# Exponentials of key tiles taken in pairs, and four elementwise steps moved from ScalarE to VectorE, in an attention and gathered-expert kernel

## Chip, cores and metric

The kernel runs on all 8 cores of one Trainium2 chip. Each core computes 4 of the 32 sequences, with no exchange between cores. The metric is the device time in microseconds of the slowest core.

## What is computed

For each sequence `x` (2048 tokens of 1024 features) a layer has two halves:

```
q = x @ Wq + bq (8 heads of 128);  k, v = x @ Wkv + bkv (one head, shared)
q += pe; k += pe
probs = softmax(causal(q k^T / sqrt(128)));  attn = probs @ v
x = layernorm(x + attn @ Wo)

grouped = x in groups of 32 tokens
logits = grouped @ Wc + bc + tie;  perm = (logits == max over the 32 tokens)
permuted = perm^T @ grouped                      (128 expert slots per group)
result = relu(permuted @ W1 + b1) @ W2 + b2, scattered back with perm
x = layernorm(x + result)
```

## The kernel before

One program is written out for five engine queues, with waits on counting semaphores; nothing is scheduled by a tool, so each engine runs its instructions in the order in which `build_nc` emits them. `wait(engine, mark)` makes the next instruction of an engine wait for a count, `gset` stores the count after which a buffer is free, and `gwait` waits for it. The loop over the 4 sequences runs these stages:

- **Projections** (L308 to L347): q, k, v for the whole sequence stay in SBUF.
- **Attention**, four blocks `qb` of 512 query rows (L451 to L547). Block `qb` uses the first 4, 8, 12 or 16 key tiles of 128 keys (`kcmax`), and its last four tiles cross the diagonal. Per head and key tile `kc`: `emit_scores` (L459) is one TensorE matmul into the PSUM bank `pp_s[kc % 2]`; `emit_exp` (L467) is a ScalarE exponential from that bank to `pT[kc % 2]`; on the four diagonal tiles VectorE multiplies `pT` by a mask (L475); `emit_pv` (L491) is four matmuls of 129 columns that add `pT` times `v` (and the row sum) into two PSUM banks. Both `pp_s` and `pT` have two buffers. Scores run two tiles ahead: in the loop of L541 to L547, `emit_pv(kc)` is followed by `emit_scores(kc + 2)` and `emit_exp(kc + 2)`.
- **End of a head**: VectorE takes four reciprocals of the row sums (L506), ScalarE scales the four 128x128 results into `pTn` (L513). TensorE transposes them (L524) after the first two score matmuls of the next head, and VectorE copies them to `atT` (L529).
- **Output projection and layernorm** at the end of each block, four row tiles of 128 tokens: 16 matmuls (L568), VectorE adds `x` (L576) and sums (L582), ScalarE squares (L586, L589), then `ln_tile` computes mean and deviation in small VectorE steps with one ScalarE square root (L382), and ScalarE applies the norm to the 128x1024 tile (L396).
- **Logits** per block: ScalarE casts the four tiles to bf16 (L417), TensorE transposes them (L426) and multiplies by `Wc` (L440).
- **Experts**, four quarters `q4` of 256 features: for each row tile `tt` ScalarE casts 256 columns of `x2` to bf16 (`x2b`, two buffers, L679), eight small matmuls gather the tokens (L690) and VectorE and ScalarE cast two results each to `gq` (L701). Then the W1 matmuls (L721), later the W2 matmuls (L775), a restack through device memory and the scatter (L831, L838). A second layernorm (L868) and the store end the sequence.

The waits that matter below are these lines of `emit_scores` and `emit_exp`:

```python
gwait("tensor", ("ps", ping))
if kc >= 2:
    wait("tensor", exp_m[kc - 2])
...
wait("scalar", sv)
gwait("scalar", ("pT", ping))
```

The first pair says that a score matmul needs its bank read by the exponential of two tiles ago. The second says that an exponential needs its scores, and that the PV matmuls of two tiles ago have read its output buffer.

Of the kernel before, what the change touches and what calls it, by code (L numbers as in the profile page):

```python
# [26 lines left out]
def build_nc(cfg):  # L27
# [88 lines left out]
    pT = [at(f"pT{i}", [128, 512], BF16, r4 + T * 2 + NT * 132 * 2 + i * 1024)  # L116
          for i in range(2)]
# [21 lines left out]
    pp_s = [nc.alloc_psum_tensor(f"pp_s{i}", [128, 512], F32).ap() for i in range(2)]  # L139
# [115 lines left out]
    def emit_ln2_finish():  # L255
        mred = now("sDVE")
        wait("scalar", mred)
        wait("scalar", now("sACT"))
        gwait("scalar", ("pT", 0)); gwait("scalar", ("pT", 1))
        for tt in range(NT):  # L260
            if tt > 0:
                wait("scalar", now("sACT"))
            inc("scalar", "sACT", 1, lambda e, tt=tt: e.activation(
                out=pT[0][:, :], in_=x2[:, tt * 1024: tt * 1024 + 512],
                func=AF.Square, accum_out=st_v[:, tt: tt + 1]))
            inc("scalar", "sACT", 1, lambda e, tt=tt: e.activation(
                out=pT[1][:, :], in_=x2[:, tt * 1024 + 512: tt * 1024 + 1024],
                func=AF.Square, accum_out=st_r[:, tt: tt + 1]))
        sq2 = now("sACT")
        gset(("pT", 0), sq2); gset(("pT", 1), sq2)  # L270
        bv = emit_ln_stats_finish()
        wait("scalar", bv)
        wait("scalar", now("sACT"))
        return bv

    for s in range(NSEQ):
# [88 lines left out]
        def ln_tile(tt, sq):  # L365
# [86 lines left out]
        for qb in range(NQB):  # L452
# [10 lines left out]
            def emit_exp(h, kc, sv, exp_m, mask_m):  # L463
                ping = kc % 2
                wait("scalar", sv)
                gwait("scalar", ("pT", ping))
                ev = inc("scalar", "sACT", 1, lambda e, ping=ping: e.activation(  # L467
                    out=pT[ping][:, :], in_=pp_s[ping][:, :], func=AF.Exp,
                    bias=c_negC, scale=cfg.SCALE))
                exp_m[kc] = ev  # L470
                gset(("ps", ping), ev)
                j = kc - 4 * qb
                if j >= 0:
                    wait("vector", ev)
                    mv = inc("vector", "sDVE", 1, lambda e, ping=ping, j=j: e.tensor_tensor(  # L475
                        pT[ping][:, :], pT[ping][:, :],
                        c_zl[:, (3 - j) * 128: (3 - j) * 128 + 512], ALU.mult))
                    mask_m[kc] = mv
# [20 lines left out]
            def emit_epilogue_pre(h):  # L499
# [54 lines left out]
            for t4 in range(4):  # L554
# [19 lines left out]
                if qb == 0 and t4 == 0 and s > 0:  # L574
# [89 lines left out]
        for q4 in range(4):  # L664
# [337 lines left out]
```

How the kernel before makes its waits and increments, by code:

```python
    def inc(eng, sem, n, buildfn):  # L160
        cnt[sem] += n; v = cnt[sem]
        emit(eng, lambda e, b=buildfn, s=sem, n=n: b(e).then_inc(sems[s], n))
        return (sem, v)
# [1 line left out]
    def wait(eng, mark):  # L165
        if mark is None: return
        sem, v = mark
        emit(eng, lambda e, s=sem, v=v: e.wait_ge(sems[s], v))
```

## Time and profile before

| | us |
|---|---|
| median of 2 runs | 5027.58 (5018.58 to 5036.58) |
| profiled execution | 5022.15 |
| its span on the slowest core | 5020.6 |
| spans of the 8 cores | 4982.2 to 5020.6 |

The profile is one execution, read on the slowest core. A busy TensorE (PE) is not an array at its peak, since its matmuls overlap and their ends are modelled. "Clock" is the TensorE clock that was granted, as a share of 2.4 GHz; it has the two levels 0.5 and 1.0, and an average over a stretch lies between. In the timeline an instruction with x2 or x4 is a run of equal ones, with the time of the whole run. "Idle before" is the time for which an engine stood before an instruction, with what ended it.

### The profile page before, as it was taken

How to read it: one execution, taken by the hardware profiler on the slowest of the kernel's cores; microseconds unless marked ns; L12 is line 12 of the kernel's file. 1: busy time of each engine (PE TensorE's matmuls, PEld its weight loads, DVE VectorE, ACT ScalarE, POOL GpSimd, SP SyncE). 2: the span in 40 equal slices, each digit the busy share in tenths (PEclk: the TensorE clock that was granted, in tenths of full speed). 3: DMA queues.
4: the chain of work that ended last, by engine and by line, in shares of the span. 5: the costliest groups of instructions: out<-in, count | busy, mean ns of one | idle time of the engine just before them, and what ended most of it. 6: DMA issues, size and time to landing. Idle time of an engine off the chain costs nothing.

```text
span 5020.6 us, 66002 instructions; the slowest of 8 cores (4982.2 to 5020.6 us)
## 1 busy us (share of the span) xinstructions
PE 2644.8 (53%) x19792; PEld 1424.3 (28%) x19792; DVE 1550.1 (31%) x4169; ACT 1883.5 (38%) x3892; POOL 18.2 (0%) x35
## 2 busy tenths in 40 slices
PE   4666664523376656462446666555426566646431
PEld 1333333311132223251113332233213223324310
DVE  1322225412232222442233212244332322134322
ACT  0345552311325556231133555433112445633313
POOL 0000000000000000000000000000000000000000
PEclk9677876555566778565566677755557678866555
DMA  4200015277400000107731000102772000010474
GB/s 87 59 13 5 18 28 125 64 163 154 118 29 14 17 18 9 68 18 168 151 105 43 17 2 17 59 35 62 156 136 97 17 17 18 1 59 35 93 160 134
DMA packets 174965, 325.00 MB, mean 65 GB/s; under 512 B 5670, under 2 KB 137126, under 8 KB 169130
## 3 DMA queue, kind: packets, MB, share of 16 engines
q1 hardware_dynamic: 26474, 164.01, 10.8%
q10 hardware_dynamic: 140224, 117.45, 10.6%
q0 software_dynamic: 7936, 39.33, 4.6%
q8 instruction: 184, 3.01, 0.2%
q14 instruction: 147, 1.20, 0.1%
HBM read 240.01 MB, written 120.07 MB: 72 GB/s over the span
## 4 chain that ended last, share of the span: by engine, by line
PE 40%; ACT 19%; DMA 17%; issue 12%; DVE 11%; ACTq 1%; DVEq 0%; SPq 0%; POOL 0%; POOLq 0%
PE pp_pv L491 8%; ACT pT L467 7%; DMA rp_scratch<-rpn 7%; DMA rpe<-rp_scratch 7%; PE pp_s L459 6%; PE pp_s L308 5%; PE pp_w L568 4%; PE pp_s L721 4%; PE pp_s L690 3%; PE pp_s L775 2%; ACT x2b L679 2%; ACT pTn L513 2%; DVE pT L475 2%; PE pp_tr L426 2%; DVE rpn L788 1%
## 5 line engine op out<-in xcount | busy, mean ns | idle before, releaser
L467 ACT ACTIVATE pT<-pp_s,c_negC 128x512 bf16<-128x512 f32 x1280 | 845.1, 690 | 350.5 <-PE pp_pv L491 210.6
L491 PE MATMUL pp_pv<-vS,pT 128*128 128x129 bf16 x5120 | 618.1, 257 | 379.5 <-DVE pT L475 229.9
L491 PEld LDWEIGHTS pp_pv<-vS,pT 128*128 128x128 bf16 x5120 | 392.8, 112 | 777.5 <-issue 773.1
L459 PE MATMUL pp_s<-qT,kT 128*128 128x512 bf16 x1280 | 599.3, 487 | 0.1
L475 DVE TENSOR_TENSOR pT<-pT,c_zl 128x512 bf16<-128x512 bf16 x512 | 217.7, 425 | 962.4 <-ACT pT L467 961.3
L775 PE MATMUL pp_s<-w_2t,inr 32*64 32x256 bf16 x1024 | 139.8, 400 | 572.6 <-DVE rpn L788 473.1
L308 PE MATMUL pp_s<-xT,w_q 128*128 128x512 bf16 x1024 | 251.2, 414 | 282.9 <-DMA w_kv<-cwkv 214.0
L788 ACT CAST rpn<-pp_s 128x256 bf16<-128x256 f32 x256 | 95.3, 372 | 700.7 <-DMA rpe<-rp_scratch 612.1
L568 PE MATMUL pp_w<-w_o,atT 128*128 128x512 bf16 x1024 | 285.4, 442 | 108.7 <-DVE x L576 94.3
L788 DVE CAST rpn<-pp_s 128x256 bf16<-128x256 f32 x256 | 108.7, 425 | 600.2 <-DMA rpe<-rp_scratch 519.7
L690 PE MATMUL pp_s<-pmt,x2b 32*128 32x128 bf16 x1024 | 128.4, 281 | 269.5 <-ACT x2b L679 259.7
L775 PEld LDWEIGHTS pp_s<-w_2t,inr 32*64 32x64 bf16 x1024 | 71.9, 122 | 638.0 <-issue 637.4
L467 ACT ACT_TABLE_LOAD x16 | 20.5, 1283 | 583.6 <-PE pp_s L459 583.6
L513 ACT ACTIVATE pTn<-pp_pv,rs 128x128 bf16<-128x128 f32 x512 | 146.1, 367 | 244.2 <-DVE rs L506 237.5
L721 PE MATMUL pp_s<-gq,w 128*32 128x64 bf16 x4096 | 228.3, 416 | 17.5 <-ACT gq L701 6.9
L701 ACT CAST gq<-pp_s 128x256 bf16<-128x256 f32 x256 | 95.2, 372 | 355.6 <-PE pp_pv L690 334.1
L308 PEld LDWEIGHTS pp_s<-xT,w_q 128*128 128x128 bf16 x1024 | 106.8, 105 | 426.0 <-issue 363.3
L721 PEld LDWEIGHTS pp_s<-gq,w 128*32 128x32 bf16 x4096 | 211.3, 144 | 32.2 <-issue 28.7
L426 PE MATMUL pp_tr<-c_ident,casttile 128*128 128x128 bf16 x512 | 74.8, 300 | 246.0 <-ACT casttile L417 169.4
L701 DVE CAST gq<-pp_s 128x256 bf16<-128x256 f32 x256 | 108.7, 425 | 262.8 <-PE pp_s L690 260.0
L679 ACT ACTIVATE x2b<-x 128x256 bf16<-128x256 f32 x256 | 109.2, 427 | 213.5 <-DVE pmT L649 120.8
L568 PEld LDWEIGHTS pp_w<-w_o,atT 128*128 128x128 bf16 x1024 | 108.2, 110 | 282.2 <-issue 212.7
(95 smaller groups left out, 3123.4 us busy)
## 6 DMA issues: line engine op xcount, KB each, us to landing
rp_scratch<-rpn SPq DMA_DIRECT2D x32, 2048.0 KB, 17.4
rpe<-rp_scratch ACTq DMA_DIRECT2D x32, 2048.0 KB, 22.4
xtile<-x SPq DMA_DIRECT2D x64, 512.0 KB, 3.7
y<-x SPq DMA_DIRECT2D x64, 512.0 KB, 4.4
w<-cw ACTq DMA_DIRECT2D x12, 2048.0 KB, 8.5
w_2t<-cw ACTq DMA_DIRECT2D x48, 512.0 KB, 13.0
xT<-xT POOLq DMA_DIRECT2D x4, 4096.0 KB, 27.6
w<-w POOLq DMA_DIRECT2D x4, 2048.0 KB, 16.2
```

The source lines that it names most:

```text
L308: mmq = inc("tensor", "sPE", 1, lambda e, ps=ps, c=c, hc=hc, tb=tb: e.matmul(ps[:, :], w_q[:, c * 1024 + hc * 128: c * 1024 + hc * 128 + 128],
L459: return inc("tensor", "sPE", 1, lambda e, kc=kc, ping=ping, h=h, qb=qb: e.matmul(pp_s[ping][:, :], kT[:, kc * 128: kc * 128 + 128], qT[:, ...
L467: ev = inc("scalar", "sACT", 1, lambda e, ping=ping: e.activation(out=pT[ping][:, :], in_=pp_s[ping][:, :], func=AF.Exp, bias=c_negC, scal ...
L475: mv = inc("vector", "sDVE", 1, lambda e, ping=ping, j=j: e.tensor_tensor(pT[ping][:, :], pT[ping][:, :], c_zl[:, (3 - j) * 128: (3 - j) * ...
L491: ping=ping, sub=sub, kc=kc, kcmax=kcmax: e.matmul(bank[:, colo: colo + 129], pT[ping][:, sub * 128: sub * 128 + 128], vS[:, kc * 132: kc ...
L513: e.activation(out=pTn[:, sub * 128: sub * 128 + 128], in_=bank[:, colo: colo + 128], func=AF.Identity, scale=rs[:, sub: sub + 1]))
L568: wv = inc("tensor", "sPE", 1, lambda e, h=h, half=half, t4=t4: e.matmul(pp_w[:, half * 512: half * 512 + 512], atT[:, h * 512 + t4 * 128: ...
L679: cm2 = inc("scalar", "sACT", 1, lambda e, tt=tt, q4=q4: e.activation(out=x2b[tt % 2], in_=x2[:, tt * 1024 + q4 * 256: tt * 1024 + q4 * 25 ...
L690: gvv = inc("tensor", "sPE", 1, lambda e, j=j, cc=cc, tt=tt, bidx=bidx: e.matmul(banks4g[bidx][:, cc * 128: cc * 128 + 128], x2b[tt % 2][j ...
L721: cc=cc, q4=q4: e.matmul(ps[b * 32: b * 32 + 32, qq * 64: qq * 64 + 64], w_1[q4 % 2][:, cc * 4096 + es * 32: cc * 4096 + es * 32 + 32], ba ...
L775: q4=q4: e.matmul(ps[half * 64: half * 64 + 64, 0:256], inr[b * 32: b * 32 + 32, q * 64: q * 64 + 64], w_2t[0][b * 32: b * 32 + 32, q * 25 ...
L788: m = inc(eng2, sem2, 1, lambda e, r=r, ps=ps, cp3=cp3: cp3(e)(rpn[:, r * 256: r * 256 + 256], ps[:, 0:256]))
```

## The change

Four things are changed:

1. `pT` and `pp_s` become the two halves of one tile each (`pTp`, `pp_sp`, 1024 columns), and one exponential of 128x1024 takes two key tiles at once (`emit_exp_pair`). It needs both score matmuls, and both halves of `pTp` free. The loop goes by pairs: two score matmuls of the next pair, then the PV matmuls of this pair, then the next exponential.
2. The scaling of the head's results (L513) goes from ScalarE to VectorE.
3. The layernorm apply after the output projection (L396) goes from ScalarE to VectorE.
4. The cast to `x2b` (L679) goes from ScalarE to VectorE.

```diff
-    pT = [at(f"pT{i}", [128, 512], BF16, r4 + T * 2 + NT * 132 * 2 + i * 1024)
-          for i in range(2)]
+    pTp = at("pTp", [128, 1024], BF16, r4 + T * 2 + NT * 132 * 2)
+    pT = [pTp[:, 0:512], pTp[:, 512:1024]]
...
-            wait("scalar", bv)
-            wait("scalar", now("sACT"))
-            am = inc("scalar", "sACT", 1, lambda e, tt=tt: e.activation(
...
-                func=AF.Identity, scale=st_r[:, tt: tt + 1], bias=st_b[:, tt: tt + 1]))
+            wait("vector", now("sDVE"))
+            am = inc("vector", "sDVE", 1, lambda e, tt=tt: e.tensor_scalar(
...
+                st_r[:, tt: tt + 1], st_b[:, tt: tt + 1], ALU.mult, ALU.add))
...
+            def emit_exp_pair(h, kc, sv, exp_m, mask_m):
                 wait("scalar", sv)
+                gwait("scalar", ("pT", 0)); gwait("scalar", ("pT", 1))
+                ev = inc("scalar", "sACT", 1, lambda e: e.activation(
+                    out=pTp[:, :], in_=pp_sp[:, :], func=AF.Exp,
                     bias=c_negC, scale=cfg.SCALE))
+                exp_m[kc] = ev; exp_m[kc + 1] = ev
+                gset(("ps", 0), ev); gset(("ps", 1), ev)
+                for k2 in (kc, kc + 1):
...
-                    nm = inc("scalar", "sACT", 1, lambda e, bank=bank, colo=colo, sub=sub:
...
+                    nm = inc("vector", "sDVE", 1, lambda e, bank=bank, colo=colo, sub=sub:
+                             e.tensor_scalar(pTn[:, sub * 128: sub * 128 + 128],
...
-                for kc in range(kcmax):
-                    epi["pv_last"] = emit_pv(h, kc, kcmax, exp_m, mask_m)
-                    nxt = kc + 2
-                    if nxt < kcmax:
-                        sv = emit_scores(h, nxt, exp_m)
-                        emit_exp(h, nxt, sv, exp_m, mask_m)
+                for kc0 in range(0, kcmax, 2):
+                    sv = None
+                    if kc0 + 2 < kcmax:
+                        emit_scores(h, kc0 + 2, exp_m)
+                        sv = emit_scores(h, kc0 + 3, exp_m)
+                    epi["pv_last"] = emit_pv(h, kc0, kcmax, exp_m, mask_m)
+                    epi["pv_last"] = emit_pv(h, kc0 + 1, kcmax, exp_m, mask_m)
+                    if sv is not None:
+                        emit_exp_pair(h, kc0 + 2, sv, exp_m, mask_m)
...
-                gwait("scalar", ("x2b", tt % 2))
-                cm2 = inc("scalar", "sACT", 1, lambda e, tt=tt, q4=q4: e.activation(
...
+                gwait("vector", ("x2b", tt % 2))
+                cm2 = inc("vector", "sDVE", 1, lambda e, tt=tt, q4=q4: e.tensor_copy(
```

The order on TensorE in the middle of a head of block 1, on tiles off the diagonal. `sACT` is ScalarE's count, `sDVE` VectorE's; L459 is a score matmul, L491 a PV matmul. Before, two buffers `pT_77` and `pT_78` take turns:

```order
L491 MATMUL pp_pv<-vS,pT_77 128x129 [waits sACT]
L491 MATMUL pp_pv<-vS,pT_77 128x129 x3
L459 MATMUL pp_s<-qT,kT 128x512 [waits sACT]
L491 MATMUL pp_pv<-vS,pT_78 128x129 [waits sACT]
L491 MATMUL pp_pv<-vS,pT_78 128x129 x3
L459 MATMUL pp_s<-qT,kT 128x512 [waits sACT]
```

And in the changed kernel:

```order
L459 MATMUL pp_sp<-qT,kT 128x512 [waits sACT] x2
L491 MATMUL pp_pv<-vS,pTp 128x129 [waits sACT]
L491 MATMUL pp_pv<-vS,pTp 128x129 x3
L491 MATMUL pp_pv<-vS,pTp 128x129 [waits sACT]
L491 MATMUL pp_pv<-vS,pTp 128x129 x3
```

The two score matmuls of the next pair now stand ahead of the eight PV matmuls of this pair, and both groups wait for the same exponential.

The order on VectorE at the end of a head of block 0 (L506 reciprocals, L475 masks, L529 the copy of the transposed result). Before:

```order
L506 RECIPROCAL rs<-pp_pv 128x1 x3
L475 TENSOR_TENSOR pT_77<-pT_77,c_zl 128x512 [waits sACT]
L475 TENSOR_TENSOR pT_78<-pT_78,c_zl 128x512 [waits sACT]
L529 COPY atT<-pp_tr 128x512 [waits sPE]
```

And in the changed kernel:

```order
L506 RECIPROCAL rs<-pp_pv 128x1 x3
L513 TENSOR_SCALAR pTn<-pp_pv,rs 128x128 [waits sDVE]
L513 TENSOR_SCALAR pTn<-pp_pv,rs 128x128 x3
L475 TENSOR_TENSOR pTp<-pTp,c_zl 128x512 [waits sACT] x2
L529 COPY atT<-pp_tr 128x512 [waits sPE]
```

The four scalings stand behind the reciprocals on VectorE, and no longer ahead of the next head's exponential on ScalarE.

The order on ScalarE in the gather stage (L679 makes `x2b` of a row tile, L701 casts gathered results). Before:

```order
L679 ACTIVATE x2b_88<-x_64 128x256 [waits sPE]
L701 CAST gq<-pp_s 128x2x128 [waits sPE]
L701 CAST gq<-pp_pv 128x2x128 [waits sPE]
L679 ACTIVATE x2b_89<-x_64 128x256 [waits sPE]
```

And on VectorE in the changed kernel, where L678 makes `x2b` and L699 casts:

```order
L678 CAST x2b_88<-x_64 128x256 [waits sPE]
L699 CAST gq<-pp_sp 128x2x128 [waits sPE]
L699 CAST gq<-pp_pv 128x2x128 [waits sPE]
L678 CAST x2b_87<-x_64 128x256 [waits sPE]
```

The cast of the next row tile stands behind two gather casts as before, but in VectorE's queue.

## Rows read from the trace of the kernel before

**Rows 1.** The page: span, and busy time of the engines.
```profile
span 5020.6 us, 66002 instructions; the slowest of 8 cores (4982.2 to 5020.6 us)
...
PE 2644.8 (53%) x19792; PEld 1424.3 (28%) x19792; DVE 1550.1 (31%) x4169; ACT 1883.5 (38%) x3892; POOL 18.2 (0%) x35
```

**Rows 2.** Windows: attention blocks 0 to 3 of the first sequence: window, busy per engine, clock.
```profile
155.00:213.00 58.00, 34.89 (x190) 17.90 (x188) 19.06 (x69) 29.69 (x61) 1.03 (x2) 0.52 0.34 91
265.00:351.00 86.00, 56.55 (x349) 29.56 (x348) 19.88 (x68) 51.08 (x93) 0.00 (x0) 0.70 0.00 1
401.00:513.00 112.00, 74.86 (x510) 39.44 (x509) 19.88 (x68) 71.89 (x125) 0.00 (x0) 0.80 0.00 1
564.00:701.00 137.00, 92.20 (x666) 49.11 (x665) 19.93 (x68) 93.11 (x157) 0.00 (x0) 0.85 0.00 1
```

**Rows 3.** Groups: instruction, shapes, count | busy us, mean ns | idle before, releaser.
```profile
L467 ACT ACTIVATE pT<-pp_s,c_negC 128x512 bf16<-128x512 f32 x1280 | 845.1, 690 | 350.5 <-PE pp_pv L491 210.6 <-PE pp_s L459 134.4 <-issue 1.0
...
L475 DVE TENSOR_TENSOR pT<-pT,c_zl 128x512 bf16<-128x512 bf16 x512 | 217.7, 425 | 962.4 <-ACT pT L467 961.3
...
L513 ACT ACTIVATE pTn<-pp_pv,rs 128x128 bf16<-128x128 f32 x512 | 146.1, 367 | 244.2 <-DVE rs L506 237.5 <-PE pp_s L459 6.7
...
L788 DVE CAST rpn<-pp_s 128x256 bf16<-128x256 f32 x256 | 108.7, 425 | 600.2 <-DMA rpe<-rp_scratch 519.7 <-PE pp_s L775 77.6
...
L396 ACT ACTIVATE x<-x,st_b,st_r 128x1024 f32<-128x1024 f32 x64 | 79.4, 1240 | 62.2 <-DVE st_b L392 62.2
...
L582 DVE TENSOR_REDUCE st_m<-x 128x1 f32<-128x1024 f32 x64 | 78.1, 1220 | 6.6
...
L417 ACT ACTIVATE casttile<-x 128x1024 bf16<-128x1024 f32 x64 | 62.0, 1039 | 0.0
```

**Rows 4.** Timeline (start, us, engine, instruction), block 3, inner loop, fast TensorE clock.
```profile
1938.81 1.26 ACT L467 ACTIVATE pT<-pp_s,c_negC 128x512 bf16<-128x512 f32 x2 [0.36 <-PE pp_pv L491]
...
1939.65 0.39 PE L491 MATMUL pp_pv<-vS,pT 128*128 128x129 bf16 x4 [0.44 <-ACT pT L467]
...
1939.88 0.38 PE L459 MATMUL pp_s<-qT,kT 128*128 128x512 bf16 x1
...
1940.41 1.26 ACT L467 ACTIVATE pT<-pp_s,c_negC 128x512 bf16<-128x512 f32 x2 [0.33 <-PE pp_s L459]
```

**Rows 5.** Timeline, block 3, inner loop, slow TensorE clock.
```profile
4341.55 0.69 ACT L467 ACTIVATE pT<-pp_s,c_negC 128x512 bf16<-128x512 f32 x1 [0.45 <-PE pp_pv L491]
...
4342.38 0.59 PE L491 MATMUL pp_pv<-vS,pT 128*128 128x129 bf16 x4
...
4342.77 0.63 PE L459 MATMUL pp_s<-qT,kT 128*128 128x512 bf16 x1
...
4343.55 0.69 ACT L467 ACTIVATE pT<-pp_s,c_negC 128x512 bf16<-128x512 f32 x1 [0.45 <-PE pp_pv L491]
```

**Rows 6.** Timeline, block 3, from the end of one head to the next.
```profile
4352.68 0.39 PE L491 MATMUL pp_pv<-vS,pT 128*128 128x129 bf16 x4 [0.48 <-DVE pT L475]
...
4353.75 1.14 ACT L513 ACTIVATE pTn<-pp_pv,rs 128x128 bf16<-128x128 f32 x4 [1.75 <-DVE rs L506]
...
4355.14 0.38 PE L524 MATMUL pp_tr<-c_ident,pTn 128*128 128x128 bf16 x4 [1.60 <-ACT pTn L513]
```

**Rows 7.** Timeline, output projection of block 3: the add that starts a tile.
```profile
2009.40 1.23 DVE L576 TENSOR_TENSOR x<-pp_w,xtile 128x1024 f32<-128x1024 f32 x1 [0.34 <-PE pp_w L568]
```

**Rows 8.** Timeline, gather stage, one row tile.
```profile
2154.12 0.49 PE L690 MATMUL pp_s<-pmt,x2b 32*128 32x128 bf16 x4 [1.03 <-ACT x2b L679]
...
2154.59 0.42 DVE L701 CAST gq<-pp_s 128x256 bf16<-128x256 f32 x1 [1.10 <-PE pp_s L690]
...
2154.93 0.41 DVE L701 CAST gq<-pp_pv 128x256 bf16<-128x256 f32 x1
...
2155.24 0.43 ACT L679 ACTIVATE x2b<-x 128x256 bf16<-128x256 f32 x1
...
2155.92 0.37 PE L690 MATMUL pp_s<-pmt,x2b 32*128 32x128 bf16 x2 [1.05 <-ACT x2b L679]
```

More of the change, by code:

```diff
@@ L137, in build_nc @@
     assert o[0] <= 224 * KB - 256, f"SBUF over: {o[0]}"
-    pp_s = [nc.alloc_psum_tensor(f"pp_s{i}", [128, 512], F32).ap() for i in range(2)]
+    pp_sp = nc.alloc_psum_tensor("pp_sp", [128, 1024], F32).ap()
+    pp_s = [pp_sp[:, 0:512], pp_sp[:, 512:1024]]
     pp_pv = [nc.alloc_psum_tensor(f"pp_pv{i}", [128, 512], F32).ap() for i in range(2)]
@@ L462, in emit_scores @@
                     start=True, stop=True))
-            def emit_exp(h, kc, sv, exp_m, mask_m):
-                ping = kc % 2
+            def emit_exp_pair(h, kc, sv, exp_m, mask_m):
                 wait("scalar", sv)
-                gwait("scalar", ("pT", ping))
-                ev = inc("scalar", "sACT", 1, lambda e, ping=ping: e.activation(
-                    out=pT[ping][:, :], in_=pp_s[ping][:, :], func=AF.Exp,
+                gwait("scalar", ("pT", 0)); gwait("scalar", ("pT", 1))
+                ev = inc("scalar", "sACT", 1, lambda e: e.activation(
+                    out=pTp[:, :], in_=pp_sp[:, :], func=AF.Exp,
                     bias=c_negC, scale=cfg.SCALE))
[L470 to L478, printed above, removed]
+                exp_m[kc] = ev; exp_m[kc + 1] = ev
+                gset(("ps", 0), ev); gset(("ps", 1), ev)
+                for k2 in (kc, kc + 1):
+                    j = k2 - 4 * qb
+                    if j >= 0:
+                        wait("vector", ev)
+                        mv = inc("vector", "sDVE", 1, lambda e, ping=k2 % 2, j=j: e.tensor_tensor(
+                            pT[ping], pT[ping],
+                            c_zl[:, (3 - j) * 128: (3 - j) * 128 + 512], ALU.mult))
+                        mask_m[k2] = mv
             def emit_pv(h, kc, kcmax, exp_m, mask_m):
@@ L506, in emit_epilogue_pre @@
                              e.reciprocal(rs[:, sub: sub + 1], bank[:, colo + 128: colo + 129]))
-                wait("scalar", rv)
-                gwait("scalar", ("pTn",))
+                wait("vector", rv)
+                gwait("vector", ("pTn",))
                 nm = None
@@ L674, in build_nc @@
                 if q4 == 0 and tt == 0:
-                    wait("scalar", pv2)
-                    if s == 0:
-                        wait("vector", st_tie); wait("scalar", st_tie)
-                gwait("scalar", ("x2b", tt % 2))
-                cm2 = inc("scalar", "sACT", 1, lambda e, tt=tt, q4=q4: e.activation(
-                    out=x2b[tt % 2], in_=x2[:, tt * 1024 + q4 * 256: tt * 1024 + q4 * 256 + 256],
-                    func=AF.Copy))
+                    wait("vector", pv2)
+                gwait("vector", ("x2b", tt % 2))
+                cm2 = inc("vector", "sDVE", 1, lambda e, tt=tt, q4=q4: e.tensor_copy(
+                    x2b[tt % 2], x2[:, tt * 1024 + q4 * 256: tt * 1024 + q4 * 256 + 256]))
                 wait("tensor", cm2)
```

25 lines of the change are left out of this document (11 added, 14 removed).

## Prediction

> **What bounds the kernel now.** I read the page first: no engine is the bound as a whole. TensorE is busy 53% of the span and ScalarE 38% [rows 1]. So the time is made of waits between engines, and the question is which wait ends last in each stage. Next I read the windows. The four attention blocks of the first sequence take 58, 86, 112 and 137 us [rows 2], 393 together and 1572 in four sequences, a third of the kernel; the biggest edit stands there. In these blocks the granted clock is 0.52, 0.70, 0.80 and 0.85, so block 0 runs at 1.2 GHz nearly throughout and block 3 mostly at 2.4 GHz.
>
> Third, the groups: the 1280 exponentials are busy 845 us with 350 us of idle time before them, which ends with a score or a PV matmul [rows 3]. So ScalarE is not full; it waits for TensorE. The timeline shows the loop that this makes. At the fast clock an exponential starts at 1938.81 and takes 0.69, the PV matmuls start at 1939.65 (0.15 after its end), the next score matmul at 1939.88 with 0.38, and the next exponential at 1940.41, 0.15 after that [rows 4]. That is 1.60 us, and since two such chains run side by side on two buffers, with the second exponential beside the matmuls of the first, 1.60 us serves two key tiles. At the slow clock the same loop takes 4341.55 to 4343.55, 2.00 us for two tiles: 0.69 + 0.14 + 0.39 + 0.63 + 0.15 [rows 5]. The reader is to see that TensorE works while ScalarE computes the other tile's exponential.
>
> **The change: the pairs.** `pTp` and `pp_sp` have two halves, but one instruction now uses both. The next pair's scores wait for this exponential, which reads both banks. The next exponential waits for this pair's PV matmuls, which read both halves. In TensorE's queue scores and PV stand between the two exponentials. Nothing runs side by side any more: exponential, wait, ten matmuls, wait.
>
> Price of the wide exponential: 128 columns from PSUM take 0.367 and 512 take 0.690 [rows 3], so 0.84 ns a column, and 1024 columns take 0.690 + 512 x 0.00084 = 1.12 us. That saves 0.26 against two of 0.69. Its bounds are 1.12 and 1.38.
>
> Price of a cycle (one pair, off the diagonal). Slow clock: exponential 1.12, wait 0.14, two score matmuls one behind the other 0.85 (512 columns at 1.2 GHz each), four PV matmuls 0.43 (516 columns), the last four 0.59 until their end, wait 0.15 [rows 5]: 3.28 us, where it was 2.00. Fast clock: 1.12 + 0.15 + 0.43 + 0.22 + 0.39 + 0.15 = 2.46 us, where it was 1.60 [rows 4].
>
> The Trainium skill ("Perfetto Trace Analysis", Optimizing Scalar/DVE Operations) says that larger operations help where the engine is saturated, and that where Scalar or Vector is not saturated but makes other engines stand still, smaller ones can let work finish earlier. The idle 350 us put this kernel in the second case, so that rule speaks against the edit, as the cycle above does.
>
> Diagonal pairs: two masks of 0.425 [rows 3] end 0.15 + 0.85 = 1.00 after the exponential, and the last four PV matmuls may start at 1.15. At the slow clock TensorE reaches them only at 0.14 + 0.85 + 0.43 = 1.42, so the masks are hidden and the cycle stays 3.28. At the fast clock they are not: 1.15 + 0.39 + 0.15 + 1.12 = 2.81.
>
> End of a head, slow clock, from the end of its last exponential: last four PV at 1.15, two scores of the next head at 1.58 and 2.01, their end 2.64 (0.63), exponential 2.79 to 3.91. Beside it runs the head's result. Before, the transposes started 2.46 us after the last PV matmuls did, with the four scalings taking 1.14 of it on ScalarE ahead of the next exponential [rows 6]. On VectorE no row shows a scaling. The cast of 256 columns from PSUM is 0.425 [rows 3]; for 128 columns the bounds are that and, with 128 columns of 0.84 ns less, 0.32. ScalarE's 0.367 lies between and I keep it, so 2.46, plus 0.20 for the slower PV matmuls. The transposes start at 1.15 + 2.66 = 3.81 and hold TensorE until 4.24; the next pair's scores could have started at 3.91 + 0.14 = 4.05. So 0.19 is added: 4.10 for the end of a head. (The bounds of the scaling make that 3.91 to 4.34, for 128 heads -24 to +30 us.) That edit by itself is a gain, since the next exponential no longer waits 1.14; it is inside the 4.10.
>
> **Which clock.** The clock is what the pairs' price hangs on. Block 0, where every tile is masked and TensorE stands still after each pair, is the stage of before whose shape is most like the new loop: it has TensorE busy 34.9 of 58 us at a clock of 0.52, while block 3 with its overlapped loop keeps 0.85 [rows 2]. The new loop leaves TensorE without work for 0.14 + 1.12 + 0.15 = 1.41 of each 3.28 us, in every block. So I take 1.2 GHz for all attention.
>
> Heads with n = 2, 4, 6, 8 pairs: 3.28 (n - 1) + 4.10 = 7.38, 13.94, 20.50, 27.06. Sum 68.9, times 8 heads 551 us, against 393. That is +158 a sequence, **+632 us** for four. Block 0 alone hardly changes (59 against 58); blocks 1 to 3 lose 26, 52 and 79.
>
> **Layernorm apply.** On VectorE it stands ahead of the next tile's add. There the add waited 0.34 for TensorE already [rows 7], so each of three gaps grows by 0.1 (a wait for its own result) + apply - 0.34. No row shows the apply on VectorE: the reduction of the same 1024 fp32 columns takes 1.22 [rows 3], with 0.1 for the two column operands 1.32. From below: the bf16 mask of 512 columns takes as long as the cast of 256 from PSUM (both 0.425), so VectorE can run at twice the rate on some operands; half of 1.22 and the 0.1 give 0.71. The ends lie near each other and I take the middle, 1.0: 3 x 0.76 = 2.3 us. In return the casts of tiles 0 to 2 no longer queue behind the last apply. Before, after the last square root came 0.97 wait (62.2/64), 1.24 apply and four casts of 0.97 (62.0/64) [rows 3], 6.1 us; now three casts cover VectorE's steps and apply, and the fourth ends at 3.9. That is -2.2. Net +0.1 a block, **+2 us** in 16 blocks (bounds -13 and +17).
>
> **x2b.** A row tile of the gather takes 2155.92 - 2154.12 = 1.80 us [rows 8]. Moved, the cast starts behind VectorE's second gather cast: 0.81 + 0.34 (the spacing of two casts) = 1.15, then its own time, then 0.25 to TensorE (2155.24 + 0.43 to 2155.92). Its own time lies between 0.425 and 0.32 (256 columns of 0.84 ns at twice the rate save 0.11); with 0.37, the middle, the tile takes 1.77. 256 x -0.03 = **-8 us** (bounds -20 and +6).
>
> The Trainium skill ("VectorE: DVE Perf Modes", What auto-detection actually checks) lets a one-source VectorE operation with both ends in SBUF run at double rate even in fp32. No row of before shows such an operation, so it stays open here. By it both steps would be at their lower bounds, and as an estimate from that page the sum would be some 30 us less than mine.
>
> **Sum.** +632 + 2 - 8 = +626 us on the profiled execution of 5022: 5648 us. The median of the runs shown is 5 us higher, which is below what I can resolve. No-change is what lies within 2%, about 100 us.
>
> **Rivals.**
> 1. *The clock holds at 2.4 GHz.* For it: block 3 holds 0.85 now, with gaps at each end of a head. Against: its loop has TensorE waiting about 0.4 us for an exponential, the new one 1.4. The end of a head becomes 1.15 + 0.22 + 0.21 + 0.38 + 0.15 + 1.12 = 3.23, plus 0.46 until the transposes (3.61 + 0.22) leave TensorE, 3.69. Heads: 2.81 + 3.69 = 6.50, then 4.92 more per step of two pairs: 11.42, 16.34, 21.26. Times 8 is 444, +51 a sequence, +205 in all: about 5220 us. A share of the time at either clock lies between.
> 2. *The wide exponential costs two narrow ones* (1.38), since it reads two banks: 640 x 0.26 = +166, about 5810 us. Against: the straight line through two widths from PSUM.
> 3. *The other side: ScalarE is the bound after all, and the kernel gets faster.* The change takes from it 640 x 0.26 = 166, L513 146, L396 79 and x2b 110, some 500 us, so about 4520 us. It decides only if the next exponential can start before the PV matmuls are through, so that a pair costs less than the 1.65 us which it costs now ((137 - 58) / 8 heads / 6 pairs). With 1.12 for the exponential and 0.3 of waits, 0.23 us would be left for ten matmuls that need 1.0 even at the fast clock. The 350 us of idle time before L467 speak against it too.
>
> **How the numbers follow.** Forecast 0.85, the fast clock through most of attention 0.07, the double-price exponential 0.05, ScalarE the bound 0.02, and 0.01 that everything cancels. The own bounds of the forecast: head ends -24 to +30, apply -13 to +17, x2b -20 to +6, and 0.05 of waits in 640 cycles, 32 either way; with a part of the windows at the fast clock down to 5500, upwards 5740. Every case but two is slower by over 2% (even rival 1 is +4%): slower 0.97, same 0.01, faster 0.02.
>
> **What would show it.** Right: 640 exponentials of 1.12 us; on the timeline no TensorE work beside them but transposes; cycles of 3.28 us off the diagonal; clock near 0.5 in all four blocks, which last 59, 112, 164 and 216 us; L513 off ScalarE. A clock of 0.7 or more in block 3 with cycles of 2.46 would make rival 1 right; exponentials of 1.38 rival 2; an exponential that starts while PV matmuls of its pair still run would make the whole forecast wrong.

## The result, and the profile after

The changed kernel takes 5643.37 us (median of 11 runs, 5631.38 to 5652.09); the kernel before takes 5022.09 us in runs beside it (10 runs, 5004.33 to 5056.12). The ratio is 1.123, 95% interval 1.1201 to 1.1259: slower by an eighth. The forecast was 5648.

First the page of the changed kernel, its span and its busy times, against [rows 1]:

```profile
span 5629.8 us, 64656 instructions; the slowest of 8 cores (5592.0 to 5629.8 us)
...
PE 2828.1 (50%) x19792; PEld 1616.6 (29%) x19792; DVE 1765.2 (31%) x5001; ACT 1461.3 (26%) x2420; POOL 18.3 (0%) x35
```

ScalarE did lose work: 1883.5 us busy became 1461.3. TensorE is busy 183 us longer with the same 19792 matmuls, but no engine got near to being full, and yet the span grew by 609 us. So the time went into slower matmuls and into waiting, and the windows say where. These are the four attention blocks of the first sequence (window, its length, then busy time and instructions of PE, PEld, DVE, ACT and POOL, the granted clock, DMA), answering to [rows 2]:

```profile
143.00:203.00 60.00, 33.39 (x197) 19.52 (x194) 25.73 (x99) 19.09 (x17) 1.03 (x2) 0.53 0.39 88
253.00:366.00 113.00, 62.95 (x350) 37.67 (x349) 26.35 (x96) 36.90 (x33) 0.00 (x0) 0.51 0.00 1
417.00:584.00 167.00, 92.87 (x509) 56.15 (x508) 26.45 (x96) 54.71 (x49) 0.00 (x0) 0.51 0.00 1
636.00:855.00 219.00, 121.78 (x663) 74.25 (x664) 25.89 (x96) 72.52 (x65) 0.00 (x0) 0.51 0.00 1
```

Blocks 0 to 3 last 59.4, 113, 167 and 220 us from the first score matmul to the last PV matmul. Blocks 1 to 3 have a clock of 0.51, where it was 0.70 to 0.85. Both show at once: longer blocks, and ScalarE and TensorE each busy for a smaller part of them. Over the four sequences the attention blocks took 1572 us before and take 2238 us after, +666. The gather stages (L690) take 419 us in place of 454, -35. The output projections, taken with the gap to the logits, are even. The q, k, v projections, which the change does not touch, are 24 us shorter in this profile (295 against 320): in the profile of before the first two of the four ran at a mean granted clock of 0.83 and 0.81 and took 86 us each, the others at 0.97 and 74; all four of after ran at 0.97 to 1.00 and 74. The clock of that stage in that execution differs, not the stage; why the chip granted it so is open. That is the balance of the 609 us.

The groups (shapes, count | busy us, mean ns | idle time before, and what ended it), against [rows 3]:

```profile
L466 ACT ACTIVATE pTp<-pp_sp,c_negC 128x1024 bf16<-128x1024 f32 x640 | 712.4, 1113 | 1464.4 <-PE pp_pv L491 1153.5 <-PE pp_sp L459 310.7
...
L459 PE MATMUL pp_sp<-qT,kT 128*128 128x512 bf16 x1280 | 651.1, 611 | 607.9 <-ACT pTp L466 607.7
...
L475 DVE TENSOR_TENSOR pTp<-pTp,c_zl 128x512 bf16<-128x512 bf16 x512 | 195.6, 422 | 1588.2 <-ACT pTp L466 1587.9
...
L513 DVE TENSOR_SCALAR pTn<-pp_pv,rs 128x128 bf16<-128x128 f32 x512 | 144.2, 344 | 24.6 <-DVE rs L506 21.8 <-PE pp_sp L459 2.7
...
L678 DVE CAST x2b<-x 128x256 bf16<-128x256 f32 x256 | 72.6, 284 | 0.0
...
L396 DVE TENSOR_SCALAR x<-x,st_r,st_b 128x1024 f32<-128x1024 f32 x64 | 52.0, 813 | 7.7 <-DVE st_b L393 1.1
```

640 exponentials of 1.113 us have 1464 us of idle time before them, most of it ended by a PV matmul; the score matmuls have 608 us before them, ended by the exponential. Each waits for the other. The loop itself, block 3 of the second sequence, against [rows 5]:

```profile
2124.36 1.11 ACT L466 ACTIVATE pTp<-pp_sp,c_negC 128x1024 bf16<-128x1024 f32 x1 [2.23 <-PE pp_pv L491]
...
2125.72 1.01 PE L459 MATMUL pp_sp<-qT,kT 128*128 128x512 bf16 x2 [1.46 <-ACT pTp L466]
...
2126.53 1.07 PE L491 MATMUL pp_pv<-vS,pTp 128*128 128x129 bf16 x8
...
2127.70 1.11 ACT L466 ACTIVATE pTp<-pp_sp,c_negC 128x1024 bf16<-128x1024 f32 x1 [2.23 <-PE pp_pv L491]
```

Between the end of the exponential at 2125.47 and the start of the next at 2127.70 ScalarE does nothing, and from the end of the PV matmuls to the next score matmul TensorE does nothing (1.46 us in the row of 2125.72). The cycle is 3.34 us for two key tiles.

The end of a head in block 2, against [rows 6]:

```profile
519.02 1.11 ACT L466 ACTIVATE pTp<-pp_sp,c_negC 128x1024 bf16<-128x1024 f32 x1 [2.23 <-PE pp_pv L491]
...
520.80 1.02 PE L491 MATMUL pp_pv<-vS,pTp 128*128 128x129 bf16 x8 [1.88 <-DVE pTp L475]
...
521.62 1.06 PE L459 MATMUL pp_sp<-qT,kT 128*128 128x512 bf16 x2
...
522.54 1.13 DVE L513 TENSOR_SCALAR pTn<-pp_pv,rs 128x128 bf16<-128x128 f32 x4 [0.18 <-DVE rs L506]
522.89 1.11 ACT L466 ACTIVATE pTp<-pp_sp,c_negC 128x1024 bf16<-128x1024 f32 x1 [2.76 <-PE pp_sp L459]
...
524.01 0.58 PE L524 MATMUL pp_tr<-c_ident,pTn 128*128 128x128 bf16 x4 [1.33 <-DVE pTn L513]
...
524.39 1.06 PE L459 MATMUL pp_sp<-qT,kT 128*128 128x512 bf16 x2
```

The last exponential of the head ends at 520.13 and the next head's first one at 524.00, 3.87 later. The transposes start at 524.01, and the score matmuls behind them at 524.39.

### The profile page after: what moved, and what is told of

It is laid out like the page before. It is cut to its first block, busy times and chain, and to the rows that moved or that the text cites. A ratio compares the mean times of both kernels' runs of the same rounds, so it can differ in the third digit from the quotient of the medians.

```text
span 5629.8 us, 64656 instructions; the slowest of 8 cores (5592.0 to 5629.8 us)
## 1 busy us (share of the span) xinstructions
PE 2828.1 (50%) x19792; PEld 1616.6 (29%) x19792; DVE 1765.2 (31%) x5001; ACT 1461.3 (26%) x2420; POOL 18.3 (0%) x35
## 3 DMA queue, kind: packets, MB, share of 16 engines
q14 instruction: 137, 1.12, 0.1%
## 4 chain that ended last, share of the span: by engine, by line
PE 42%; ACT 17%; DVE 15%; DMA 15%; issue 9%; DVEq 1%; SPq 0%; ACTq 0%; POOL 0%; POOLq 0%
ACT pTp L466 11%; PE pp_pv L491 10%; PE pp_sp L459 9%; DMA rp_scratch<-rpn 6%; DMA rpe<-rp_scratch 6%; PE pp_sp L309 4%; PE pp_sp L719 3%; PE pp_w L569 3%; DVE pTn L513 3%; PE pp_sp L688 2%; PE pp_sp L773 2%; DVE gq L699 2%; DVE x L577 1%; PE pp_tr L426 1%; DVE rpn L786 1%
## 5 line engine op out<-in xcount | busy, mean ns | idle before, releaser
L466 ACT ACTIVATE pTp<-pp_sp,c_negC 128x1024 bf16<-128x1024 f32 x640 | 712.4, 1113 | 1464.4 <-PE pp_pv L491 1153.5
L459 PE MATMUL pp_sp<-qT,kT 128*128 128x512 bf16 x1280 | 651.1, 611 | 607.9 <-ACT pTp L466 607.7
L491 PE MATMUL pp_pv<-vS,pTp 128*128 128x129 bf16 x5120 | 679.4, 313 | 241.3 <-DVE pTp L475 241.3
L491 PEld LDWEIGHTS pp_pv<-vS,pTp 128*128 128x128 bf16 x5120 | 577.5, 145 | 468.3 <-issue 438.6
L475 DVE TENSOR_TENSOR pTp<-pTp,c_zl 128x512 bf16<-128x512 bf16 x512 | 195.6, 422 | 1588.2 <-ACT pTp L466 1587.9
L773 PE MATMUL pp_sp<-w_2t,inr 32*64 32x256 bf16 x1024 | 140.1, 400 | 576.2 <-DVE rpn L786 483.4
L309 PE MATMUL pp_sp<-xT,w_q 128*128 128x512 bf16 x1024 | 230.9, 390 | 283.6 <-DMA w_kv<-cwkv 214.5
L459 PEld LDWEIGHTS pp_sp<-qT,kT 128*128 128x128 bf16 x1280 | 139.3, 113 | 779.4 <-issue 721.5
L699 ACT CAST gq<-pp_sp 128x256 bf16<-128x256 f32 x256 | 95.2, 372 | 617.5 <-PE pp_pv L688 588.1
L719 PE MATMUL pp_sp<-gq,w 128*32 128x64 bf16 x4096 | 223.8, 408 | 18.3 <-ACT gq L699 11.7
L719 PEld LDWEIGHTS pp_sp<-gq,w 128*32 128x32 bf16 x4096 | 206.6, 142 | 33.6 <-issue 29.8
L699 DVE CAST gq<-pp_sp 128x256 bf16<-128x256 f32 x256 | 108.8, 425 | 186.5 <-PE pp_sp L688 183.2
```

The costliest lines, as they stand in the source:

```text
L309: mmq = inc("tensor", "sPE", 1, lambda e, ps=ps, c=c, hc=hc, tb=tb: e.matmul(ps[:, :], w_q[:, c * 1024 + hc * 128: c * 1024 + hc * 128 + 128],
L459: return inc("tensor", "sPE", 1, lambda e, kc=kc, ping=ping, h=h, qb=qb: e.matmul(pp_s[ping][:, :], kT[:, kc * 128: kc * 128 + 128], qT[:, ...
L466: ev = inc("scalar", "sACT", 1, lambda e: e.activation(out=pTp[:, :], in_=pp_sp[:, :], func=AF.Exp, bias=c_negC, scale=cfg.SCALE))
L475: mv = inc("vector", "sDVE", 1, lambda e, ping=k2 % 2, j=j: e.tensor_tensor(pT[ping], pT[ping], c_zl[:, (3 - j) * 128: (3 - j) * 128 + 512 ...
L491: ping=ping, sub=sub, kc=kc, kcmax=kcmax: e.matmul(bank[:, colo: colo + 129], pT[ping][:, sub * 128: sub * 128 + 128], vS[:, kc * 132: kc ...
L699: m = inc(eng2, sem2, 1, lambda e, g=g, bidx=bidx, cp2=cp2: cp2(e)(bass.AP(gq.tensor, gq.offset + g * 128, [[gq.ap[0][0], 128], [NG * 128, ...
```

## Experiments

The attention time in this table is the sum of the 16 blocks in the profiled run, each from its first score matmul to its last PV matmul, read from the timeline. Each time is a median, of 4 runs for runs 1 to 8 and of 10 for run 9. Ratios are against the kernel before, in runs on the same chip; it took 5022 us beside the changed kernel, 5018 beside runs 1 to 4, 5017 beside 5 to 7 and 5008 beside 8 and 9, so differences of some 10 us between rows are not resolved.

| run | us | ratio, 95% interval | attention, us |
|---|---|---|---|
| before | 5022 | 1 | 1572 |
| changed | 5643 | 1.123 (1.120 to 1.126) | 2238 |
| 1 moves alone | 4936 | 0.983 (0.980 to 0.986) | 1537 |
| 2 pairs alone | 5749 | 1.145 (1.142 to 1.149) | 2302 |
| 3 changed, single wait | 5603 | 1.117 (1.113 to 1.121) | 2193 |
| 4 changed, fillers | 5276 | 1.052 (1.048 to 1.057) | 1875 |
| 5 changed, two narrow exponentials | 5727 | 1.141 (1.136 to 1.145) | 2327 |
| 6 changed, two output buffers | 5174 | 1.030 (1.026 to 1.035) | 1769 |
| 7 changed, both sides double | 4492 | 0.896 (0.891 to 0.901) | 1098 |
| 8 apply and x2b moved alone | 4972 | 0.993 (0.991 to 0.995) | 1565 |
| 9 as 6, with fillers | 5029 | 1.003 (1.001 to 1.006) | 1624 |

### 1 and 2: the two halves of the change

The change moves three elementwise steps, not the four of the title: the scaling, the apply and `x2b`. Run 1 is the kernel before with these three edits. Run 2 is the changed kernel with them undone; the part of the scaling is:

```diff
-                wait("vector", rv)
-                gwait("vector", ("pTn",))
+                wait("scalar", rv)
+                gwait("scalar", ("pTn",))
...
-                    nm = inc("vector", "sDVE", 1, lambda e, bank=bank, colo=colo, sub=sub:
-                             e.tensor_scalar(pTn[:, sub * 128: sub * 128 + 128],
+                    nm = inc("scalar", "sACT", 1, lambda e, bank=bank, colo=colo, sub=sub:
+                             e.activation(out=pTn[:, sub * 128: sub * 128 + 128],
```

> The kernel before with the three moves to VectorE alone (scaling, apply, x2b), key tiles one by one as before. My theory: the moves gain. At the end of a head the next exponential no longer stands behind four scalings, so the next head's PV matmuls start right behind the transposes, 0.25 to 0.8 us earlier, some -65 us over 128 heads; the gather's row tile takes 1.69 in place of 1.80 us, -30 us; the apply is even. About 4930 us against 5022. Rival: all that the moves free is idle time of ScalarE, and the time stays within 1%. Second rival: VectorE's queue gets late, and it is slower.

Measured 4936 against 5018.

> The changed kernel with the three moves undone, so the pairs alone. My theory: the loss is the pair loop, so it shows in full, and more than in the changed kernel: each next head's wide exponential waits behind the scalings on ScalarE again (+0.6 us, 128 heads, +77) and the gather is as it was (+34): about 5755 us. Rival: part of the loss came from work put on VectorE (masks behind scalings), and the time is below 5643.

Measured 5749. So the moves gain 82 us by themselves and the pairs lose 732; together they lose 621. On top of the pairs the moves are worth 106, more than alone. The gather stages give 35 us of it in either case; attention gives 64 on top of the pairs and 35 alone. That a wide exponential which waits for four scalings holds up two tiles would fit this, but no run separates it. The rivals do not hold: what ScalarE was freed of was not all idle time, and the work moved to VectorE shortens the run with the pairs and without them, so it is not the source of the loss.

### 3: one of two waits taken out

```diff
                 gwait("tensor", ("ps", ping))
-                if kc >= 2:
-                    wait("tensor", exp_m[kc - 2])
```

Both waits are for the same count, so nothing is left unguarded.

> The changed kernel without the second of two waits for the same count ahead of a score matmul. In the trace the score matmuls start 0.25 us after the exponential's end, where PV matmuls with a single wait started 0.14 us after it. If the second wait costs the difference: the cycle goes from 3.34 to 3.24 us, 640 times, -60 us, about 5580. If the 0.25 is the latency of this hand-over whatever the number of waits: 5643, no change.

Measured 5603, -40 us; the four runs (5593 to 5617) all lie below the eleven of the changed kernel (5631 to 5652). The timeline of this run, same loop:

```profile
2112.37 1.11 ACT L464 ACTIVATE pTp<-pp_sp,c_negC 128x1024 bf16<-128x1024 f32 x1 [2.12 <-PE pp_pv L489]
...
2113.63 1.01 PE L457 MATMUL pp_sp<-qT,kT 128*128 128x512 bf16 x2 [1.36 <-ACT pTp L464]
...
2115.60 1.11 ACT L464 ACTIVATE pTp<-pp_sp,c_negC 128x1024 bf16<-128x1024 f32 x1 [2.12 <-PE pp_pv L489]
```

The exponential ends at 2113.48 and the score matmul starts at 2113.63: 0.15 us, where the changed kernel has 2125.47 to 2125.72, 0.25 us. The cycle is 3.23 in place of 3.34. The second wait did cost 0.10 us, in each cycle. The saving is below the 60 us expected because I multiplied by all 640 exponentials. The second wait is written only for `kc >= 2`, so the first pair of each of the 128 heads never had it. 512 x 0.10 = 51, of which the attention time shows 45 and the run 40.

### 4: fillers

```diff
                     epi["pv_last"] = emit_pv(h, kc0 + 1, kcmax, exp_m, mask_m)
+                    if kc0 + 2 < kcmax:
+                        for _i in range(3):
+                            emit("tensor", lambda e, h=h, qb=qb: e.matmul(
+                                pp_trf0[:, :], kT[:, 0:128],
+                                qT[:, h * T + qb * 512: h * T + qb * 512 + 512],
+                                start=True, stop=True, skip_group_check=True))
```

> The changed kernel with three extra score-sized matmuls of 512 columns into an unused PSUM bank after each pair's PV matmuls (where another pair follows); nobody waits for them, and they fill the time in which TensorE waits for the exponential (1.28 of 1.36 us at the slow clock). If the clock is a cause of its own: it rises to 1.0 in blocks 1 to 3, the cycle falls from 3.34 to about 2.57 us, and the time falls to 5250 to 5350 us though more work is done. If the clock stays at 0.5, or TensorE's rate is not what sets the cycle: 5643 or more.

Measured 5276, -367 us, with 1536 matmuls more to do. Windows of blocks 1 and 3 (as above):

```profile
248.00:346.00 98.00, 60.59 (x423) 31.76 (x422) 27.58 (x104) 37.00 (x33) 0.00 (x0) 0.91 0.00 1
...
582.00:763.00 181.00, 117.99 (x841) 62.26 (x840) 27.81 (x104) 72.60 (x65) 0.00 (x0) 0.94 0.00 1
```

The clock is 0.91 and 0.94, where it was 0.51. The loop in block 3, with the fillers in `pp_trf`:

```profile
702.61 0.81 PE L550 MATMUL pp_trf<-qT,kT 128*128 128x512 bf16 x3
702.88 1.11 ACT L466 ACTIVATE pTp<-pp_sp,c_negC 128x1024 bf16<-128x1024 f32 x1 [1.41 <-PE pp_pv L491]
...
704.24 0.61 PE L459 MATMUL pp_sp<-qT,kT 128*128 128x512 bf16 x2 [0.81 <-ACT pTp L466]
...
705.40 1.11 ACT L466 ACTIVATE pTp<-pp_sp,c_negC 128x1024 bf16<-128x1024 f32 x1 [1.41 <-PE pp_pv L491]
```

The cycle is 2.52 us. Nothing was removed from it; the same ten matmuls take less time (the two score matmuls 0.61 us where they took 1.01). So of the loss, 367 us hang on the clock that the waiting TensorE was granted, and some 255 (5276 against 5022, with the gain of the moves inside) are left for the loop near the fast clock.

### 5: two narrow exponentials

```diff
-                ev = inc("scalar", "sACT", 1, lambda e: e.activation(
-                    out=pTp[:, :], in_=pp_sp[:, :], func=AF.Exp,
-                    bias=c_negC, scale=cfg.SCALE))
+                for half in range(2):
+                    ev = inc("scalar", "sACT", 1, lambda e, half=half: e.activation(
+                        out=pT[half], in_=pp_s[half], func=AF.Exp,
+                        bias=c_negC, scale=cfg.SCALE))
```

> The changed kernel, each wide exponential written as two of 512 columns one behind the other, with the waits and the order as they are. My theory: width is the one thing in the pair edit that saves time. Two narrow ones take 1.26 us together (as the pairs of the kernel before did), the wide one 1.11: +0.15 us in 640 cycles, +96, about 5740 us. Rival: reading two banks in one instruction costs the hand-over (the 0.25 us before the score matmuls), and the time stays or falls.

Measured 5727, +84 us, and +89 in the attention time. The wide instruction is a gain, 0.14 us each, and the loss stays when it is taken back, so its width is not what costs. The rival (a cost of reading two banks at once) is out. What does cost, the buffers that the pair takes, is tested in run 6.

### 6 and 9: two output buffers, then with fillers

```diff
+    pTq = at("pTq", [128, 1024], BF16, r7)
+    pTP = [pTp, pTq]
...
-                gwait("scalar", ("pT", 0)); gwait("scalar", ("pT", 1))
+                b2 = (kc // 2) % 2
+                gwait("scalar", ("pT", 2 * b2 + 1))
```

`r7` holds tiles that are not in use during a block's heads.

> The changed kernel with two output buffers of 1024 columns for the exponential, in turn; the score banks stay one pair. The next exponential then waits for its scores alone, and PV runs beside it. Theory: cycle at the slow clock 1.11 + 0.25 + 0.43 + 0.63 + 0.15 = 2.57 in place of 3.34 us, 512 cycles within heads (four blocks of 8 heads with 1, 3, 5, 7), -394 us, about 5250 us, or less where the clock rises. It says that the lost second buffer is what costs. Rival: the shared score banks alone cost, and the second output buffer gives under 50 us.

Measured 5174, -469 us. The loop where the clock is slow:

```profile
701.57 1.01 PE L461 MATMUL pp_sp<-qT,kT 128*128 128x512 bf16 x2 [0.65 <-ACT pTq L470]
...
702.38 1.07 PE L495 MATMUL pp_pv<-vS,pTq 128*128 128x129 bf16 x8
...
702.74 1.11 ACT L470 ACTIVATE pTp<-pp_sp,c_negC 128x1024 bf16<-128x1024 f32 x1 [1.41 <-PE pp_pv L495]
...
704.10 1.01 PE L461 MATMUL pp_sp<-qT,kT 128*128 128x512 bf16 x2 [0.65 <-ACT pTp L470]
```

The exponential of 702.74 starts 0.36 us after the first PV matmul of 702.38 and 0.16 after the end of the two score matmuls (701.57 + 1.01): it no longer waits for its predecessor's PV matmuls, which run beside it until 703.45, though the view still names L495 as what ended its wait. The cycle is 2.53 us, for the 2.57 expected. The run is 76 us below the forecast of 5250; 512 x 0.04 = 20 us of that are the shorter cycle, and the rest fits a loop that runs at the fast clock part of the time (block 3 has a mean granted clock of 0.66). The second expectation was about that part:

> The kernel with two exponential output buffers (5174 us, block 3 at a clock of 0.67), plus two filler matmuls of 512 columns per pair into an unused bank. It separates the lost score buffer from the clock: if the clock goes to about 0.9 in the blocks, the cycle is 1.11 + 0.25 + 0.21 + 0.38 + 0.15 = 2.10 us, and the time 5000 to 5080 us. If the part that was left at the slow clock was not what held it, 5174 or more.

Measured 5029, 1.003 of the kernel before. Two exponentials of this run, one cycle:

```profile
702.06 1.11 ACT L470 ACTIVATE pTq<-pp_sp,c_negC 128x1024 bf16<-128x1024 f32 x1 [1.01 <-PE pp_pv L495]
...
704.21 1.11 ACT L470 ACTIVATE pTp<-pp_sp,c_negC 128x1024 bf16<-128x1024 f32 x1 [1.03 <-PE pp_pv L495]
```

2.15 us, near the 2.10 of the sum. The profiled execution is the slowest of the ten (5061 us; five of them took 5014 to 5020): its q, k, v projections ran on this core at a granted clock of 0.80 to 0.84 and took 86 us each, where run 6 has 73. The attention time, which this does not touch, went from 1769 to 1624, 52 above the kernel before, and the gather stages give 35 of that back. With one pair of score banks, a second output buffer and a clock near the fast one (0.93 in block 3) the change is a draw.

### 7: both sides double

On top of run 6 the score pairs alternate between two bank pairs, and scores run two pairs ahead:

```diff
+                if kc % 4 < 2:
+                    gwait("tensor", ("ps", kc % 2)); dst = pp_s[kc % 2]
+                else:
+                    gwait("tensor", ("pw", kc % 2))
+                    dst = pp_w[:, (kc % 2) * 512: (kc % 2) * 512 + 512]
...
+                for kc0 in range(0, kcmax, 2):
+                    epi["pv_last"] = emit_pv(h, kc0, kcmax, exp_m, mask_m)
+                    epi["pv_last"] = emit_pv(h, kc0 + 1, kcmax, exp_m, mask_m)
+                    if kc0 + 4 < kcmax:
+                        emit_scores(h, kc0 + 4, exp_m)
+                        sv = emit_scores(h, kc0 + 5, exp_m)
+                        emit_exp_pair(h, kc0 + 4, sv, exp_m, mask_m)
```

> As the run with two output buffers, and the score pairs also alternate between two pairs of PSUM banks (pp_w, which is idle during a block's heads, is the second), with scores two pairs ahead. Theory: both sides are buffered as in the kernel before, but with wide exponentials and the three moves. A pair off the diagonal costs about 1.2 us at the fast clock (ScalarE nearly full) against 1.65 before, on the diagonal about 1.6. Blocks of some 37, 58, 77 and 96 us, about 4500 us in all: faster than both kernels. Rival: TensorE's clock or the ends of heads eat it, and it stays at or above 4936, the time of the moves alone.

Measured 4492, ratio 0.896 (0.891 to 0.901): faster than both kernels. The blocks last 36.5, 59.9, 78.8 and 99.3 us (means of the four sequences). The loop in block 3:

```profile
563.02 1.11 ACT L471 ACTIVATE pTp<-pp_sp,c_negC 128x1024 bf16<-128x1024 f32 x1 [0.34 <-PE pp_sp L462]
...
563.28 0.59 PE L462 MATMUL pp_w<-qT,kT 128*128 128x512 bf16 x2
564.04 1.11 ACT L471 ACTIVATE pTq<-pp_w,c_negC 128x1024 bf16<-128x1024 f32 x1
...
564.28 0.61 PE L497 MATMUL pp_pv<-vS,pTp 128*128 128x129 bf16 x8 [0.41 <-ACT pTp L471]
...
565.48 1.11 ACT L471 ACTIVATE pTp<-pp_sp,c_negC 128x1024 bf16<-128x1024 f32 x1 [0.34 <-PE pp_sp L462]
```

Two exponentials every 2.46 us (563.02 to 565.48), so 1.23 us for two key tiles, with `pp_sp` and `pp_w` in turn; the second of each two starts before the first is written down as ended. The window of block 3:

```profile
470.00:572.00 102.00, 71.13 (x672) 41.51 (x670) 28.24 (x105) 69.44 (x65) 0.00 (x0) 0.98 0.00 1
```

The clock is 0.98 with no fillers: in this loop, which keeps TensorE fed, the clock stays up too.

One thing stays open. The kernel before has two key tiles in flight, in two score banks and two output buffers; run 7 has four. So its gain over the moves alone (4936 to 4492) is not the wide instruction's alone. Run 5 puts the width at 84 us in the serial loop; what narrow exponentials with four banks and four buffers would do was not run.

### 8: which of the moves gains

Run 1 with the scaling put back on ScalarE.

> The kernel before with two moves, apply and x2b, and the scaling left on ScalarE. Against the run of all three moves (4936) it tells which of them gains. Theory: x2b -34 us and apply +-0, so about 4985 us; the other 50 us of the three moves are the scaling's, by a next head that starts earlier. Rival: the scaling gives nothing, and this one too is at 4936.

Measured 4972 (0.993, 0.991 to 0.995). Apply and `x2b` give some 36 us of the 82, the scaling the other 46. The two profiled executions differ by 28 us, all of it in the attention time (1565 and 1537); where the rest of the 46 lies is open. Most of the 28 is in the four blocks 0, which last 53 us in place of 58. In block 2 the scaling on VectorE gains under 1 us, and the granted clock there is lower than with the scaling on ScalarE (0.77 against 0.85). The rival (scaling gives nothing) is out.

## Why the prediction was right

**The pair cycle.** The step was 3.28 us at the slow clock; the loop shows 3.34. The one term of the cycle that was mis-sized is the wait ahead of the score matmul, taken as 0.14 from a PV matmul [rows 5] and measured as 0.25; the other terms together came out 0.05 shorter (1.11 for 1.12, and 1.98 for 2.02 from the first score matmul to the next exponential). Run 3 shows why: a score matmul had two waits written ahead of it, a PV matmul one. Together 512 x 0.06 = 31 us more than forecast. It is most of the 34 us by which the attention blocks (+666) passed the forecast (+632).

**The wide exponential.** 1.12 from the line through two widths; 1.113 measured. Run 5 confirms the sign. The saving of 0.26 that the prediction names is a misreading, which only rivals 2 and 3 use: two exponentials of 0.69 one behind the other take 1.26 together, as the row of 1938.81 shows [rows 4], and run 5 measures 0.14.

**The masks** were hidden at the slow clock: block 0, where every pair is masked, takes 59.4 us against the 59 forecast with unmasked cycles, and from block to block the time grows by the same 54 us, 3.35 a cycle.

**The end of a head** was 3.91 us to the end of the next head's first exponential, and 3.87 measured; the transposes were to hold up the next pair's scores until 4.24, and those scores start 4.26 after (524.39 - 520.13). The scaling on VectorE costs 0.344, between the bounds and near ScalarE's 0.367 that I kept.

**The clock** was taken as the slow one throughout, by the likeness to block 0. A granted clock of 0.51 to 0.55 in all 16 blocks confirms it, and run 4 shows that it is a cause and not a mere sign: the same loop at a high clock is 367 us faster. That block 0 foretells the clock of the other three was an analogy, with no more than one block to rest on. Rival 1, the fast clock, was priced at 5220 with a cycle of 2.46; the fillers bring 5276 with 2.52, so the price of the cycle was good and only the condition did not hold. The rest of that price is not confirmed: its attention time is 1777 us, run 4 has 1875, at a clock of 0.73 to 0.82 in block 0 and with no fillers at the ends of heads.

**The apply.** Three gaps were to grow by 0.76 each against a saving of 2.2. The rows, against [rows 7]:

```profile
2306.80 0.15 DVE L393 TENSOR_SCALAR st_b<-st_b 128x1 f32<-128x1 f32 x1
2307.06 0.81 DVE L396 TENSOR_SCALAR x<-x,st_r,st_b 128x1024 f32<-128x1024 f32 x1
2307.79 1.22 DVE L577 TENSOR_TENSOR x<-pp_w,xtile 128x1024 f32<-128x1024 f32 x1
```

It takes 0.81 us, below the 1.0 I took, and the next add starts behind it without a wait. Three casts of one run go beside VectorE's steps and the fourth behind the last apply, as described:

```profile
2311.62 0.29 ACT L383 ACTIVATE st_v<-st_v,c_eps 128x1 f32<-128x1 f32 x1 [1.08 <-DVE st_v L379]
2311.82 2.93 ACT L417 ACTIVATE casttile<-x 128x1024 bf16<-128x1024 f32 x3
...
2312.82 0.81 DVE L396 TENSOR_SCALAR x<-x,st_r,st_b 128x1024 f32<-128x1024 f32 x1
...
2314.66 1.04 ACT L417 ACTIVATE casttile<-x 128x1024 bf16<-128x1024 f32 x1
```

Over the 16 blocks the projection stage is 25 us longer and the gap from it to the logits 28 us shorter: nothing in sum, where +2 was forecast. With the measured 0.81 the prediction's own working gives -8; where the difference lies is open.

**x2b** gained more than forecast. The step had -8 us with 0.37 us for the cast. The rows, against [rows 8]:

```profile
2406.26 0.49 PE L688 MATMUL pp_sp<-pmt,x2b 32*128 32x128 bf16 x4 [0.94 <-DVE x2b L678]
...
2407.07 0.41 DVE L699 CAST gq<-pp_pv 128x256 bf16<-128x256 f32 x1
...
2407.40 0.28 DVE L678 CAST x2b<-x 128x256 bf16<-128x256 f32 x1
...
2407.93 0.49 PE L688 MATMUL pp_sp<-pmt,x2b 32*128 32x128 bf16 x4 [0.90 <-DVE x2b L678]
```

The cast takes 0.28, and the row tile 1.67 (2406.26 to 2407.93) in place of 1.80: 256 x 0.13 = 33 us, which is -33 and outside the bounds given (-20 and +6). For both moved operations I had taken the middle of the bounds. The cast came out below its lower bound (0.28 against 0.32), the apply nearer its lower than its upper one (0.81 between 0.71 and 1.32). The Trainium skill ("VectorE: DVE Perf Modes", What auto-detection actually checks) says that a one-source operation within SBUF can run at double rate in fp32 too. The trace fits this and does not prove it: the apply moves 1024 columns in 0.81 us, where the reduction needs 1.22, and with one width the fixed part is not told from the rate. The estimate from that page, some 30 us less for the two steps, meets their sum (-35), but not its parts: it has -13 and -20, where the stages show 0 and -35.

**The sum.** The pair loop was 34 us too low, these two steps some 30 too high. The two errors cancelled, which is luck, and without it the forecast would still have been within 1%. The 5 us are between the forecast and the median. The profiled execution is 17 below the forecast (5631), and there the 24 us of the q, k, v projections, which nobody forecast, are in it.

**The rivals.** The double-price exponential is refuted by 1.113 us. ScalarE as the bound is refuted by the page of the profile: it lost 422 us of work (the prediction had some 500, with 166 for the exponentials, whose busy time fell by 133), and the kernel got slower. The Trainium skill ("Perfetto Trace Analysis", Optimizing Scalar/DVE Operations) says that breaking up instructions may let work finish sooner where Scalar or Vector is not saturated and makes other engines stand still. As a warning against this change it came out right, but run 5 does break up the exponential, with the waits left as they are, and is 84 us slower. The waits that came with the width cost, not the width; in run 7 the same wide operation stands in the fastest kernel.

## What to carry to other kernels

Merging two instructions that worked in turn on two buffers also merges the buffers: write down, before the edit, which waits stand between one such instruction and the next, and give the merged one two buffers on each side. A loop that becomes serial may also lose TensorE's clock, and then pays twice; here that was more than half of the loss (367 of 621 us), and the loop with full buffers got it back by itself. Of the three steps moved to VectorE two paid, the cast to `x2b` and the scaling that stood ahead of the next head's exponential; the apply gave nothing.

## What the runs showed of the hardware that I had not expected

- A second wait for a count that is already covered by the first cost 0.10 us on TensorE (0.25 against 0.15 us from the end of the exponential to the score matmul, run 3).
- Matmuls that nobody needs paid: 1536 of them, fitted into TensorE's waiting time, took 367 us off (run 4), through a granted clock of 0.91 to 0.94 in place of 0.51.
- A VectorE cast of 256 fp32 columns to bf16 within SBUF took 0.284 us, against 0.425 from PSUM, and an fp32 scale and add of 1024 columns within SBUF 0.813 us (L678, L699 and L396 of the changed kernel).
